# Moving a block's finish on VectorE and GpSimd behind the next block's norm in both chains of a four-layer cross-attention kernel

## The reference

```python
# layer 0, behind its self-attention                      (chain 0)
x = x + softmax(ln2(x) Wq . K(ctx)) V(ctx) Wo + bo        # "ca", 16 heads x 64 context rows
x = x + gelu(ln3(x) W1 + b1) W2 + b2                      # "mlp"
# layer 1: a gated update of x by routed context tokens
routed = softmax(x . tok / 16) tok
ps, inn = ln(x), ln(routed)
u, r = sigmoid([ps, inn] Wu + bu), sigmoid([ps, inn] Wr + br)
cand = tanh([r * ps, inn] Wn + bn)
x = ln((1 - u) * x + u * cand)                            # "n6": the finish of chain 0

# layer 2, behind its self-attention                      (chain 2)
x = x + softmax(ln2(x) Wq . K(ctx)) V(ctx) Wo + bo        # "cb"
p = ln3(x) W1 + b1; x = x + (p[:1024] * gelu(p[1024:])) W2 + b2   # "ff"
# layer 3
out = ln(x + softmax(x Wq . K(ctx)) V(ctx) Wo)            # "cc", then "n10": the finish of chain 2
```

## Time and profile before

| | |
|---|---|
| median of the runs | 2376.32 us |
| the profiled execution's own time | 2376.05 us |
| its span in the profile | 2374.3 us |
| TensorE (PE) busy | 2087.5 us (88%) |
| VectorE (DVE) busy | 1119.0 us (47%) |
| ScalarE (ACT) busy | 932.2 us (39%) |
| GpSimd (POOL) busy | 776.8 us (33%) |
| granted TensorE clock, mean | 0.945 of full speed |

### The profile page before, as it was taken

How to read it: one execution, slowest core, us unless ns; L and a number is a source line. 1 busy time by engine, 2 the same in 40 slices (tenths; PEclk the granted TensorE clock), 3 DMA queues, 4 the chain that set the end, 5 groups by cost and what they waited for, 6 DMA issues and landing times. The chain is left out here.

```text
span 2374.3 us, 27271 instructions
## 1 busy us (share of the span) xinstructions
PE 2087.5 (88%) x10510; PEld 1202.8 (51%) x10550; DVE 1119.0 (47%) x2012; ACT 932.2 (39%) x1435; POOL 776.8 (33%) x508
## 2 busy tenths in 40 slices
PE   3789998487979767999999999999998989898987
PEld 1444444275757554433343335334433857676766
DVE  5377662435252435455535554555450143535343
ACT  2246666133323222555545553554455322122211
POOL 3211100013032120566646664666466010202011
PEclk8899999799989887999999999999999989898989
DMA  5822420400000004000000000000000510000000
GB/s 115 131 39 38 51 29 2 113 1 0 1 0 0 1 1 122 1 1 1 1 1 1 1 1 1 1 1 2 1 2 1 161 28 1 9 1 9 0 9 9
DMA packets 48266, 52.77 MB, mean 22 GB/s; under 512 B 14730, under 2 KB 39052, under 8 KB 47732
## 3 DMA queue, kind: packets, MB, share of 16 engines
q1 hardware_dynamic: 48148, 51.17, 10.3%
HBM read 41.31 MB, written 8.80 MB: 21 GB/s over the span
## 5 line engine op out<-in xcount | busy, mean ns | idle before, releaser
L1734 POOL TENSOR_TENSOR total<-total,pr 128x1024 f32<-128x1024 f32 x192 | 464.9, 2421 | 241.9 <-ACT pr L1875 229.0
L1875 ACT ACTIVATE pr<-sc 128x1024 f32<-128x1024 f32 x256 | 259.7, 1021 | 355.6 <-PE sc L1654 355.6
L1755 DVE TENSOR_REDUCE pmax<-ring 128x1 f32<-128x512 f32 x512 | 325.8, 684 | 133.9 <-PE ring L1621 126.9
L1672 PE MATMUL o<-pr,v_pair 128*64 128x512 f32 x1024 | 275.7, 617 | 1.2
L1654 PE MATMUL sc<-q_full,k_full 64*128 64x512 f32 x1024 | 267.1, 591 | 0.0
L522 ACT ACTIVATE probs<-s 128x512 f32<-128x512 f32 (+1 forms) x304 | 163.2, 575 | 102.3 <-PE s L309 55.7
L1621 PE MATMUL ring<-k_round,q_round 64*128 64x512 f32 x512 | 185.0, 598 | 5.2 <-DVE pmax L1755 4.3
L1030 POOL TENSOR_TENSOR c_scores<-c_scores,c_total 128x1024 f32<-128x1024 f32 (+1 forms) x48 | 77.0, 1614 | 338.3 <-DVE c_total L986 338.3
L1621 PEld LDWEIGHTS ring<-k_round,q_round 64*128 64x128 f32 x512 | 74.4, 188 | 155.2 <-DVE pmax L1755 97.2
L394 DVE TENSOR_REDUCE row_max<-s 128x1 f32<-128x640 f32 (+3 forms) x128 | 127.3, 1020 | 47.4 <-PE s L291 47.1
L1672 PEld LDWEIGHTS o<-pr,v_pair 128*64 128x64 f32 x1024 | 51.2, 134 | 144.2 <-issue 142.4
(11 more groups left out here) (286 smaller groups left out, 3421.9 us busy)
## 6 DMA issues: line engine op xcount, KB each, us to landing
qk_dram<-qk_parts SPq DMA_DIRECT2D x32, 192.0 KB, 3.0
q_stack<-qk_dram SPq DMA_DIRECT2D x48, 128.0 KB
k_stack<-qk_dram SPq DMA_DIRECT2D x48, 128.0 KB
x<-in_x SPq DMA_DIRECT2D x4, 512.0 KB, 7.5
mlp_w<-in_L_xattn_mlp_w SPq DMA_DIRECT2D x2, 1024.0 KB, 8.3
wq<-in_L_xattn_Wq SPq DMA_DIRECT2D x2, 1024.0 KB, 6.5
wo<-in_L_xattn_Wo SPq DMA_DIRECT2D x2, 1024.0 KB, 14.9
hT<-in_L_xattn_ff_w SPq DMA_DIRECT2D x1, 2048.0 KB, 19.0
```

What stands on the lines that cost most here:

```text
L1672: ins = te.matmul(o[64 * j:64 * j + 64], v[n % 2][:, kt, 64 * j:64 * j + 64], probs[(U * n + u) % KEPT][:, j], start=kt == 0, stop=kt == T ...
L1734: pool.tensor_tensor(out=total[half][:], in0=other[:], in1=probs[at % KEPT][:], op=ALU.add).then_inc(sums, 1)
L1755: dve.tensor_reduce(part_max[:, j, t, half:half + 1], ring[i % RING][:], AX.X, ALU.max).then_inc(s1_free, 1)
L1875: act.activation(probs[here % KEPT][:], s2[at % 2][:], ACT.Exp).then_inc(s2_free, 1)
```

## The change

In `emit` of both chains, VectorE's `finish_block(i - 1)` moves from ahead of the loop over the streams, in which the cross attention's output is added and normed, to behind it. GpSimd's share of the finish (`n6`, `n10`) moves behind its share of `n3` (`n9`), so that both engines keep one order. The finish of block 3, at the end of a chain, stays where it is. No instruction is added, removed or changed in size.

```diff
@@ part_chain0, vector
                 cross_vector(dve, ch, "ca", i, 1024)
+                for s in range(B):
+                    add_vector(dve, ch, e, "ca.x", i, "ca.out", s, bank=1)
+                    norm_vector(dve, ch, "n3", i, x, lambda s: after_spare(dve, ch, s, "ca.x", i), streams=[s])
                 if not first:
                     finish_block(i - 1)
-                for s in range(B):
-                    add_vector(dve, ch, e, "ca.x", i, "ca.out", s, bank=1)
-                    norm_vector(dve, ch, "n3", i, x, lambda s: after_spare(dve, ch, s, "ca.x", i), streams=[s])
@@ part_chain0, gpsimd
                 cross_gpsimd(pool, ch, "ca", i, 1024)
+                norm_gpsimd(pool, ch, e, "n3", i)
                 if not first:
                     norm_gpsimd(pool, tail, e, "n6", i - 1)
-                for name in ("n3", "n4", "n5"):
+                for name in ("n4", "n5"):
                     norm_gpsimd(pool, ch, e, name, i)
@@ part_chain2, vector
                 cross_vector(dve, ch, "cb", i, 1024)
+                for s in range(B):
+                    add_vector(dve, ch, e, "cb.x", i, "cb.out", s)
+                    norm_vector(dve, ch, "n9", i, x, lambda s: after_spare(dve, ch, s, "cb.x", i), streams=[s])
                 if not first:
                     finish_block(i - 1, not isinstance(i, int) or i > 1)
-                for s in range(B):
-                    add_vector(dve, ch, e, "cb.x", i, "cb.out", s)
-                    norm_vector(dve, ch, "n9", i, x, lambda s: after_spare(dve, ch, s, "cb.x", i), streams=[s])
@@ part_chain2, gpsimd
                 cross_gpsimd(pool, ch, "cb", i, 1024)
+                norm_gpsimd(pool, ch, e, "n9", i)
                 if not first:
                     norm_gpsimd(pool, tail, e, "n10", i - 1)
-                norm_gpsimd(pool, ch, e, "n9", i)
```

More of the change, by code:

```diff
@@ L1287, in emit @@
                 cross_vector(dve, ch, "ca", i, 1024)
-                if not first:
-                    finish_block(i - 1)
                 for s in range(B):
@@ L1292, in emit @@
                     norm_vector(dve, ch, "n3", i, x, lambda s: after_spare(dve, ch, s, "ca.x", i), streams=[s])
+                if not first:
+                    finish_block(i - 1)
                 for s in range(B):
@@ L2216, in emit @@
                 cross_vector(dve, ch, "cb", i, 1024)
-                if not first:
-                    finish_block(i - 1, not isinstance(i, int) or i > 1)
                 for s in range(B):
@@ L2221, in emit @@
                     norm_vector(dve, ch, "n9", i, x, lambda s: after_spare(dve, ch, s, "cb.x", i), streams=[s])
+                if not first:
+                    finish_block(i - 1, not isinstance(i, int) or i > 1)
                 for half in range(2):
```

## The result

The changed kernel takes 2345.24 us (median of 4 runs, 2343.8 to 2346.3) against 2376.38 us before: ratio 0.9867, 95% interval 0.985 to 0.9884, so 1.3% faster. A second set of runs gave 2344.39 us and 0.9863 (0.9849 to 0.9878). The forecast was 2342.2 us with a range of 2337 to 2349; the saving was 31.1 us where 34.1 were expected. The profiled execution took 2344.33 us. Two kernels further down, e8 and e11, each had one much longer run with a lower granted clock (2559.86 and 2394.51 us), which their medians of six runs count and their ratios leave out.

The account below looks back on a forecast made before the run. VectorE's in-order finish ahead of stream 0's add and norm was taken as the limit. Savings of 24.4 us (chain 0) and 9.6 us (chain 2) made 34.1 us off 2376.05, giving 2342.2 us, range 2337 to 2349.

Parts of the forecast that it names:

- The limit is VectorE's order: At block boundaries VectorE does the finish before stream 0's add and norm, so TensorE idles 5.63 us (chain 0) or 1.31 us.
- Block 0 as the measure: Block 0 has no finish ahead of its norm; its 5.83 and 5.82 us from L883 to the up matmuls sized the saving.
- The clock's share: At the six boundaries, 13.3 of the 34.1 us come from matmuls and transposes running at the higher clock.
- The cover of the finish: Behind stream 1's norm the 6.2 us finish costs nothing: 13.4 us to spare in chain 0, 1.0 in chain 2.
- Time to spare for stream 0: In chain 0, stream 0's `h` is ready at 694.03, 0.5 us before TensorE comes to the transposes.
- The sum: The savings at the three boundaries of chain 0 and the three of chain 2 together make 34.1 us.
- The term "chain 0": Blocks 1 to 3 of chain 0 come down to block 0's stretch: 7.81, 7.95 and 8.68, together 24.4 us.
- The term "chain 2": Block 2 of chain 2 exceeds block 0 by 3.21 us; taken for each of three boundaries, 9.6 us.
- The stores: SyncE's stores of `result` go out some 7 us later in blocks 1 to 3; the last block's are not touched.
- The first: Rival: the clock falls at the boundaries all the same, only 20.8 us come back, 2355.5 us; chance 0.11.
- the second: Rival: the change does nothing because another wait ends where VectorE's did, 2376 us; chance 0.03.
- the third: Rival: the moved finish holds up chain 2's gated product, time 2342 + 3 × (overrun − 4.6) us; chance 0.03.

Follow-up runs that it names:

- e8: e7's kernel with the same fill of TensorE's waits also in chain 2's second cross attention; 2322.58 us, ratio 0.9761 to the kernel before.
- e11: The kernel of e8 run once more, unchanged; 2321.27 us, ratio 0.9768 to the kernel before.
- e4: The changed kernel with the finish between the norms of stream 0 and stream 1, in both chains; 2361.52 us, ratio 0.9941 to the kernel before.
- e3: The kernel before, old order kept, with extra unused matmuls filling TensorE's wait for stream 0's normed values; 2367.78 us, ratio 0.9965.
- e5: The changed kernel with 3 extra reductions on VectorE behind the finish in blocks 1 to 3 of chain 2; 2344.54 us, ratio 0.9864 to the kernel before.
- e6: The changed kernel with 7 extra reductions on VectorE behind the finish in blocks 1 to 3 of chain 2; 2355.76 us, ratio 0.9913 to the kernel before.
- e7: The changed kernel with repeated transposes and extra matmuls in two TensorE waits of every block's first cross attention; 2321.74 us, ratio 0.9773 to the kernel before.
- e10: The kernel of e7 run once more, unchanged; 2323.72 us, ratio 0.9777 to the kernel before.
- e1: The change in chain 0 alone, chain 2 as in the kernel before; 2353.12 us, ratio 0.9904 to the kernel before.

## Why the prediction was right, and where its size was off

- *The limit is VectorE's order.* Right: the waits of 5.6 and 1.3 to 1.4 us for `h` are gone. e4 shows that each stream's values have a time of their own.
- *Block 0 as the measure.* Right at all six boundaries: 5.82 us where 5.83 and 5.82 were read. This is the step that sized the saving; idle time alone would have given 20.8 us, and the forecast from it, 2355.5 us, is 10 us off.
- *The clock's share.* Right in kind and place: e3 gives the clock back without moving anything on VectorE. The gap of 1.11 us did not lower the clock in any of the eight blocks.
- *The cover of the finish.* Right: 0.93 us left against 1.0 in chain 2, 13.37 against 13.4 in chain 0, and 4.67 us of free overrun against 4.6 (e5, e6).
- *Time to spare for stream 0.* Expected 0.5 us, measured 0.24. The interval from the copy's end to L883 is the same as before (3.8 us), but the transposes start 0.12 us behind L883's start and not at its modelled end, and the add starts 0.05 us behind the copy.
- *The sum.* 34.1 us expected, 31.1 measured. The six stretches that it adds up gave 34.2; what it lacked lies outside them. The term "chain 0" (24.4 expected) is 23.0 and 23.6 us in two profiles, because the parts between the boundaries together took 1.5 and 0.9 us more than before. The prediction foresaw that as spread, at 1.3 us a block; in these profiles such a part takes from 90.6 to 92.7 us. The term "chain 2" (9.6 expected) is 10.0. The rest is the 1.7 us at the end of chain 2, where a stretch at the low clock now falls into TensorE's last matmuls; before, these ran at 1.00 to their end. The prediction had no term for it, and that the range held it is owed to the room left for other causes. The Trainium skill ("TensorE: Matmul & The Clock Gate", section "What's actually happening") says that the monitor's window runs freely. The trace agrees in so far as waits of 1.25 or 1.26 us and 1.17 or 1.18 us are followed by 1.99 us at the full clock in some blocks and by 2.83 to 3.68 us in others, and even in one block of one kernel by 3.43 us in one profile (e7, block 2) and by 1.99 in the other (e10).
- *The stores.* The text has them go out some 7 us later. In chain 2, block 2 the finish ended 1.96 us ahead of the start of L883 and now ends 10.15 us behind it, so it is 12 us; nothing waits for them there.
- *The rivals.* The first (low clock all the same), the second (no effect) and the third (slower) did not occur. e6 shows that the third is real as a mechanism, with the price that was given for it.

## What to carry to other kernels

Look for a block, a first or a last one, in which the work in question is absent: its stretch measures idle time and clock at once, which a sum of waits doesn't. On an engine that works in order, put work that nobody waits for behind the last instruction that somebody does, and check the next wait behind it for room. Where TensorE waits for a few microseconds in a chain, count the matmuls behind the wait as well; harmless repeated work in the wait can give these back their speed (some 2.9 us a block behind two waits of 1.98 and 2.18 us in chain 2).

## What the runs showed of the hardware that was not expected

- A single wait of 1.11 us between full stretches left TensorE at 2.4 GHz in all eight blocks of the changed kernel; waits of 1.31 to 1.41 and 1.11 us with 0.66 us of transposes between them were each time (three blocks each in the kernel before and in e1) followed by 16 matmuls of 5.41 us instead of 3.72. Waits of 1.26 and 1.17 us with 0.66 us of work between them are on the edge: from 1.99 to 3.68 us for 8 matmuls, by kernel and block. In two profiles of the changed kernel the values are the same (2.84 and 2.88 us in blocks 2 and 3), in two of e7's kernel they are not. What decides it is not shown.
- A stretch at the low clock can move instead of being added: in the changed kernel 8 matmuls lost 0.85 us and the 8 transposes behind them 0.87, and 32 matmuls further on gained 1.7.
- More work on TensorE made the kernel faster: e7's fill took some 22 us off, though it only put work where TensorE had waited.
